# Moving half of the first attention phase of an eight-phase transformer kernel into the chunks of the phase behind it

## What is computed

```python
x = x + tanh(g_xattn[0]) * xattn0(layernorm(x), ctx)      # phase 0
x = x + tanh(g_ffn[0]) * ffn0(layernorm(x), Wr, Wg, Wu, Wd)   # phase 1

def xattn0(Q, K):                 # per block; no softmax
    scores = tril(ones) * (K @ K.T)
    return Q + scores @ Q

def ffn0(x, Wr, Wg, Wu, Wd):      # 8 experts of 256 hidden, top 2
    combine = softmax over the top 2 of x @ Wr, scattered to 8
    return sum over e of (silu(x @ Wg[e]) * (x @ Wu[e]) @ Wd[e]) * combine[e]
```

## Time and profile before

| | |
|---|---|
| median of 3 runs | 873.83 us |
| the runs | 873.89, 866.33, 873.83 us |
| the profiled execution | 869.13 us, of which its span is 867.3 us |
| TensorE busy | 824.7 us, 95% of the span |
| VectorE, ScalarE, GpSimd busy | 515.7, 407.0, 471.2 us |
| mean granted TensorE clock | 0.985 of full speed |

### The profile page before, as it was taken

The page is one execution under the profiler, slowest core; times in us unless marked ns, Lnnn a source line. Parts: engine busy times, 40 slices in busy tenths (PEclk is TensorE's granted clock), DMA queues, the critical chain, the costliest instruction groups (busy, mean ns, idle before and its releaser), DMA issues.

```text
span 867.3 us, 13578 instructions
## 1 busy us (share of the span) xinstructions
PE 824.7 (95%) x4427; PEld 560.2 (65%) x4427; DVE 515.7 (59%) x1444; ACT 407.0 (47%) x730; POOL 471.2 (54%) x449
## 2 busy tenths in 40 slices
PE   5999999998899999999998999999999988999997
PEld 5866676665566666665765666656566665666664
DVE  6866645584865646335555868686755466556431
ACT  2343353634436242325666676756556633424231
POOL 5585757465573747476444343354545248475553
PEclk9999999999999999999999999999999899999999
DMA  8303111214313142441323131322223024424251
GB/s 317 104 15 99 63 36 32 85 43 154 119 44 119 62 129 67 136 124 35 89 83 107 46 89 42 95 50 50 55 49 93 1 67 134 147 66 148 75 154 50
DMA packets 44727, 75.29 MB, mean 87 GB/s; under 512 B 8977, under 2 KB 9361, under 8 KB 44529
## 3 DMA queue, kind: packets, MB, share of 16 engines
q1 hardware_dynamic: 44512, 74.42, 28.4%
q10 hardware_dynamic: 144, 0.01, 0.0%
HBM read 56.11 MB, written 1.51 MB: 66 GB/s over the span
## 4 chain that ended last, share of the span: by engine, by line
PE 56%; DVE 9%; ACT 3%; issue 2%; POOL 0%; ACTq 0%; DVEq 0%; POOLq 0%
PE Y L930 13%; PE B L857 6%; PE B L855 6%; PE B L856 6%; PE B L1498 5%; PE B L1517 3%; PE B L1479 3%; PE B L1485 2%; PE Y L1370 2%; PE B L1478 2%; DVE mxh L1768 1%; PE T L1303 1%; DVE xhat L1752 1%; DVE bcs L1943 1%; ACT shared L1379 1%
## 5 line engine op out<-in xcount | busy, mean ns | idle before, releaser
L1172 POOL TENSOR_TENSOR shared<-shared,bcs 128x512 f32<-128x512 f32 x192 | 247.4, 1293 | 195.8 <-DVE shared L1209 177.0
L1209 DVE TENSOR_TENSOR shared<-shared,B 128x512 f32<-128x512 f32 x204 | 139.5, 686 | 206.4 <-PE B L857 160.4
L1058 ACT ACTIVATE shared<-B 128x512 f32<-128x512 f32 x204 | 121.7, 598 | 280.0 <-PE B L857 279.5
L930 PE MATMUL Y<-shared,down_lo 128*128 128x512 f32 x408 | 209.1, 598 | 0.0
L1712 POOL TENSOR_TENSOR shared_r<-shared_r,const 128x512 fp32r<-128x512 f32 (+1 forms) x128 | 116.4, 940 | 80.3 <-PE B L1479 61.8
L1768 DVE TENSOR_REDUCE mxh<-B 128x4 fp32r<-128x512 f32 (+1 forms) x128 | 78.9, 618 | 82.2 <-PE B L1479 81.5
L1648 ACT COPY shared<-B 128x512 f32<-128x512 f32 (+1 forms) x128 | 64.7, 505 | 61.6 <-PE B L1498 61.5
L1638 ACT ACTIVATE shared<-B 128x512 f32<-128x512 f32 (+1 forms) x128 | 69.6, 544 | 48.9 <-PE B L1485 47.6
L930 PEld LDWEIGHTS Y<-shared,down_lo 128*128 128x128 f32 x408 | 72.5, 190 | 21.1 <-issue 9.5
L855 PE MATMUL B<-shared_r,gate_hi 128*128 128x512 f32 x102 | 80.9, 794 | 0.0
L855 PE MATMUL B<-x_lo_r,gate_hi 128*128 128x512 f32 x102 | 77.6, 761 | 0.4 <-ACT shared L1058 0.4
(11 more groups left out here) (306 smaller groups left out, 1469.8 us busy)
## 6 DMA issues: line engine op xcount, KB each, us to landing
bcs<-wrow SPq DMA_DIRECT2D x96, 256.0 KB, 3.8
shared_r<-shared_r SPq DMA_DIRECT2D x256, 64.0 KB, 2.0
bcs<-wrow SPq DMA_DIRECT2D x128, 128.0 KB, 2.9
gate_lo<-in_moe SPq DMA_DIRECT2D x9, 256.0 KB, 5.3
up_lo<-in_moe SPq DMA_DIRECT2D x9, 256.0 KB, 5.5
down_lo<-in_moe SPq DMA_DIRECT2D x9, 256.0 KB, 4.3
small<-in_small SPq DMA_DIRECT2D x1, 1372.5 KB, 11.7
X<-in_x SPq DMA_DIRECT2D x4, 256.0 KB, 5.2
```

What stands on the lines that cost most here:

```text
L930: nc.tensor.matmul(Y[:], w_raw[2][:, at:at + P], hid[(n0 + c) % HIDDEN], start=(i == 0), stop=(i == m["NC"] - 1))\
L1058: nc.scalar.activation(sg[(n0 + n) % ACTIVE], B[n % GATES][:], ACT.Silu).then_inc(sem("sg_ready"), 1)
L1172: gp.tensor_tensor(hid[(n0 + n) % HIDDEN], hid[(n0 + n) % HIDDEN], bcs[(PLACE.k0[p] + r // m["PER"]) % BROADCAST], ALU.mult)\
L1209: nc.vector.tensor_tensor(hid[(n0 + n) % HIDDEN], sg[(n0 + n) % ACTIVE], up[:], ALU.mult)\
```

## The change

Groups 0 and 1 of phase 0 stay in front of the first chunk; groups 2 and 3 move inside the first seven chunks of phase 1. On PE the scores of group 2 come behind chunk 0 and its result behind chunk 2, the scores of group 3 behind chunk 3 and its result behind chunk 5. Both use bank B5 for the scores and Y for the result. The normalising of groups 1, 2 and 3 goes from DVE to ACT (`p0_apply`: an activation with a scale and a bias for each partition, four for a group), for which DVE also writes the negated mean and POOL multiplies it by the inverse root (`offset0`). The casts of pieces 2 and 3 move behind the first four SiLUs on ACT; the subtractions of pieces 2 and 3 move from DVE to POOL, the last of them behind weighted chunks 1 and 2. POOL's four tiles of group 1 (`apply(run.step(1), ...)`) move from ahead of the chunks to one behind each of weighted chunks 0 to 3. The gate and up weights of each piece are loaded right behind the group's context, and the down weights behind all of them with semaphores of their own.

```diff
-        xhat0, sm = ([area0.tile([P, TG]) for g in range(NG)] for _ in range(2))
+        xhat0, sm = ([area0.at_tile(i + g, [P, TG]) for g in range(NG)] for i in (15, 19))
...
+        neg_mean0 = sb("neg_mean0", [P, NG, GB])
+        offset0 = sb("offset0", [P, NG, GB])
+        SCORE0, OUT0 = (B[0], B[1], B[5], B[5]), (Y, B[4], Y, Y)
+
+        def p0_scores(pe, g):
+            pe.wait_ge(sem(f"ctx_loaded{g}"), 16)
+            if g == 3:
+                pe.wait_ge(sem("p0_masked"), 3)
+            for j in range(GB):
+                kt = context(g, j)
+                ins = nc.tensor.matmul(SCORE0[g][:, j * P:(j + 1) * P], kt, kt, start=True, stop=True)
+            ins.then_inc(sem("p0_scores"), 1)
+
+        def p0_result(pe, g):
+            pe.wait_ge(sem("p0_masked"), g + 1)
+            pe.wait_ge(sem("p0_xhat"), g + 1)
+            if g >= 2:
+                pe.wait_ge(sem("p0_updated"), (1, 3)[g - 2])
+            for j in range(GB):
+                o, q = OUT0[g][:, j * P:(j + 1) * P], xhat0[g][:, j * P:(j + 1) * P]
+                nc.tensor.matmul(o, sm[g][:, j * P:(j + 1) * P], q, start=True, stop=False)
+                ins = nc.tensor.matmul(o, ident, q, start=False, stop=True)
+            ins.then_inc(sem("p0_out"), 1)
...
-            for g in range(NG):
-                scores(g)
-            result(0)
-            result(1)
+            p0_scores(pe, 0)
+            p0_scores(pe, 1)
+            p0_result(pe, 0)
+            p0_result(pe, 1)
             norm_pe(pe, 0, 0)
-            result(2)
             pe.wait_ge(sem("first_loaded"), 16)
             route_pe(pe, 1)
-            result(3)
...
+            if g:
+                v.tensor_scalar(neg_mean0[:, g, :], mv0[:, g, :, 0], -1.0, None, ALU.mult)
+            v.tensor_scalar(var0[:, g, :], mv0[:, g, :, 1], LN_EPS, None, ALU.add).then_inc(sem("p0_var"), 1)
...
-            statistics(0)
-            statistics(1)
-            apply(0)
-            mask(0)
-            apply(1)
-            mask(1)
-            statistics(2)
+            p0_statistics(dve, st, 0)
+            p0_mask(dve, 0)
+            dve.wait_ge(sem("p0_rstd"), 1)
+            for j in range(GB):
+                ins = nc.vector.tensor_scalar(xhat0[0][:, j * P:(j + 1) * P], token_tile(0, j),
+                                              mv0[:, 0, j, 0:1], rstd0[:, 0, j:j + 1], ALU.subtract, ALU.mult)
+            ins.then_inc(sem("p0_xhat"), 1)
+            p0_statistics(dve, st, 1)
+            p0_mask(dve, 1)
             dve.wait_ge(sem("tgate_ready"), 1)
-            update(0)
+            p0_update(dve, 0)
             norm_stats(st, 0)
-            statistics(3)
             norm_apply(dve, 0, 0, 0)
-            apply(2)
-            mask(2)
-            apply(3)
-            mask(3)
+            p0_statistics(dve, st, 2)
             x_low_dve(dve, 1)
-            update(1)
-            update(2)
+            p0_update(dve, 1)
             for _ in route_dve(dve, st, 1):
                 pass
-            update(3)
+
...
+        def p0_apply(act, g):
+            act.wait_ge(sem("p0_offset"), g)
+            if g == 1:
+                act.wait_ge(sem("p0_xhat"), 1)
+            for j in range(GB):
+                ins = nc.scalar.activation(xhat0[g][:, j * P:(j + 1) * P], token_tile(g, j), ACT.Identity,
+                                           bias=offset0[:, g, j:j + 1], scale=rstd0[:, g, j:j + 1])
+            ins.then_inc(sem("p0_xhat"), 1)
 
         def p0_act(act):
-            for q in range(2):
-                for k in range(2):
-                    weights_hi(act, 1, q, k)
+            p0_apply(act, 1)
+            for k in range(2):
+                weights_hi(act, 1, 0, k)
             norm_act(act, 0, 0)
             x_high_act(act, 1)
             for k in range(2):
-                weights_hi(act, 1, 2, k)
+                weights_hi(act, 1, 1, k)
             scores_act(act, 1)
-            for k in range(2):
-                weights_hi(act, 1, 3, k)
...
+                if g:
+                    pool.wait_ge(sem("p0_rstd"), g + 1)
+                    gp.tensor_tensor(offset0[:, g, :], neg_mean0[:, g, :], rstd0[:, g, :], ALU.mult)\
+                        .then_inc(sem("p0_offset"), 1)
 
             power0(0)
             power0(1)
-            power0(2)
+            power(0)
             for k in range(2):
                 weights_lo(pool, gp, 1, 0, k, "w_lo1")
-            power(0)
+            power0(2)
+            for q in (1, 2):
+                for k in range(2):
+                    weights_lo(pool, gp, 1, q, k, "w_lo1")
             power0(3)
-            pool.wait_ge(sem("p0_masked"), NG)
-            for k in range(2):
-                weights_lo(pool, gp, 1, 1, k, "w_lo1")
...
-                    if i == a and p == 1 and q >= 2:
-                        pe.wait_ge(sem("w_lo1_dve"), 2 * (q - 1))
-                    elif i == a:
+                    if i == a:
                         pe.wait_ge(sem(f"w_lo{p}"), 2 * (q + 1))
...
+                    if p == 1 and n in (0, 3):
+                        p0_scores(pe, 2 + n // 3)
                     if (p, n) == (1, 2):
                         turn(1, 0)
+                    if p == 1 and n in (2, 5):
+                        p0_result(pe, 2 + n // 5)
...
-                if (p, n) == (1, 1):
+                if (p, n) == (1, 2):
                     turned_act(act, 1)
...
+                if p == 1 and n in (0, 4):
+                    p0_apply(act, 2 + n // 4)
+                if p == 1 and n < 4:
+                    weights_hi(act, 1, 2 + n // 2, n % 2)
...
-            apply(run.step(1), range(GB))
+            if run is STREAMS[1]:
+                apply(run.step(1), range(GB))
...
+                if p == 1 and n < GB:
+                    apply(run.step(1), (n,))
+                if p == 1 and n in (1, 2):
+                    weights_lo(pool, gp, 1, 3, n - 1, "w_lo1")
...
-                norm_stats(st, 1)
...
-                if p == 1 and n in (1, 2, 3, 4):
-                    weights_lo(dve, nc.vector, 1, 2 + (n - 1) // 2, (n - 1) % 2, "w_lo1_dve")
+                if p == 1 and n in (1, 4):
+                    p0_mask(dve, 2 + n // 4)
+                if p == 1 and n in (3, 6):
+                    p0_update(dve, 2 + n // 6)
+                if (p, n) == (1, 1):
+                    norm_stats(st, 1)
+                if (p, n) == (1, 2):
+                    p0_statistics(dve, st, 3)
...
                 sp.dma_start(CT[:, c], ctx_d[:, c]).then_inc(sem(f"ctx_loaded{g}"), 16)
+                for k in range(2) if g else ():
+                    sp.dma_start(w_raw[k][:, piece(1, g - 1)], moe_d[1][k][:, piece(1, g - 1)])\
+                        .then_inc(sem(f"raw1_{g - 1}"), 16)
+            for k in range(2):
+                sp.dma_start(w_raw[k][:, piece(1, 3)], moe_d[1][k][:, piece(1, 3)]).then_inc(sem("raw1_3"), 16)
             for q in range(NG):
-                for k in range(3):
-                    sp.dma_start(w_raw[k][:, piece(1, q)], moe_d[1][k][:, piece(1, q)]).then_inc(sem(f"raw1_{q}"), 16)
+                sp.dma_start(w_raw[2][:, piece(1, q)], moe_d[1][2][:, piece(1, q)]).then_inc(sem(f"raw_down1_{q}"), 16)
```

78 lines of the change are left out of this document (28 added, 50 removed).

## The result

| | kernel before | kernel changed |
|---|---|---|
| median of 22 runs each, taken in turn | 873.12 us | 877.0 us |
| ratio of the times, 95% interval | | 1.0049, 1.0028 to 1.007 |
| the profiled execution, its span | 869.13, 867.3 us | 876.9, 875.1 us |
| mean granted TensorE clock | 0.985 | 0.983 |
| transposes of group 1 begin | 44.11 us | 48.05 us |

The change costs 4.3 us by the ratio (2.4 to 6.1); the two medians are 3.9 us apart. The forecast was 873 us, level with the kernel before, and it expected the transposes of group 1 at 45.9. They come 3.95 us later than before instead of 1.8.

The account below looks back on a forecast made before the run. TensorE was taken to bound the kernel, with gaps at the start. A 7.6 us lead less 5.4 us of returned work and later waits came to +1.8 us: 870.9 or 875.6, middle 873 us, range 866 to 879.

Parts of the forecast that it names:

- Until chunk 0: Start of the kernel: with group 0 alone first and apply at 1.1 us, chunk 0 at 19.9 us against 27.53.
- T1: Start of the transposes of group 1 in the one profiled execution; forecast at 45.9 us against 44.11.
- 16.8 and 19.9: Start of the kernel: forecast times in us of the transposes of group 0 and of chunk 0's first matmul.
- the tiles' 1.04 us: Price of one GpSimd normalising tile when VectorE works beside it, against 0.81 us alone.
- The routing: VectorE's step behind x_lo and update of group 1: 3.2 us, VectorE free at 23.8, SiLU 0 at 24.0.
- PE's wait for the result of group 2: Behind chunk 2 and the transposes of comb: PE stands 2.0 us until VectorE's mask of group 2 at 28.5.
- GpSimd's tiles last: Ahead of group 1's transposes: tiles ready at 45.9, PE waits 1.9 us, +1.8 us; as a rival, +0.5 to +3.5, chance 0.50.
- The two unmeasured prices: Operations without a trace row: ACT's four 128x128 activations, 1.55 us together, and POOL's 4-column offset, 0.5 us.
- The table load: Between ACT's exponential and SiLU 0: 1.28 us with nothing behind it; by the skill's drain, 1.4 us more.
- rival 3: Clock falls again in waits ahead of group 2's result or for the tiles: +4.0 us, 877 on forecast's scale; chance 0.13.
- The level: Base for the +1.8 us: 870.9 from the profiled execution, 875.6 from the median; the middle, 873 us, was predicted.

Follow-up runs that it names:

- e1_hold: Changed kernel plus one wait: GpSimd's subtractions of weight piece 0 wait for VectorE's normalised x of group 0; 875.9 us, ratio 1.0045 to the kernel before.
- h2_after_ride_held: Changed kernel plus one wait in phase 3: GpSimd waits until VectorE has written the riding attention's four tiles; 868.76 us, ratio 0.9948 to the kernel before.
- f1: Kernel before without GpSimd's wait for the four phase 0 masks ahead of piece 1's subtractions; 877.94 us, ratio 1.0041 to the kernel before.
- g4: Kernel before plus one wait in phase 3: GpSimd waits until VectorE has written the riding attention's four tiles; 866.48 us, ratio 0.9899 to the kernel before.
- k2: The same kernel as g4, run again on another chip; 868.27 us, ratio 0.9931 to the kernel before.
- g1: f3 with GpSimd's subtractions of pieces 0 and 1 back where the changed kernel has them, without waits for VectorE; 872.33 us, ratio 0.9975 to the kernel before.
- f3: Changed kernel with its start reordered on GpSimd, ScalarE, TensorE and VectorE, with subtractions held apart from VectorE's normalising; 867.93 us, ratio 0.9927 to the kernel before.
- f2: e2 with one VectorE setup copy rewritten to read PSUM and the other moved to an earlier step; 872.71 us, ratio 0.9992 to the kernel before.
- e2: Changed kernel with GpSimd's four tiles of group 1 back ahead of the weighted chunks; 881.31 us, ratio 1.0093 to the kernel before.
- e3: Changed kernel plus 19 unread 128x128 matmuls in TensorE's idle time around the transposes of group 0; 878.71 us, ratio 1.0073 to the kernel before.
- e4: Changed kernel with the normalising of groups 2 and 3 back on VectorE, behind products 0 and 4; 881.02 us, ratio 1.0109 to the kernel before.
- h1_probe: Kernel before plus three stretches behind its end of twelve back-to-back GpSimd instructions each, beside VectorE work; ran once, 912.82 us, no ratio.

## Why the prediction was wrong

- **Until chunk 0: the failed step.** "Update, statistics, power and apply then take what they took." The apply was priced at the 1.1 us of the earlier trace rows, which it had beside a mere power (18.35 us, four columns), the subtractions being over by 16.86. The change itself set the subtractions on the same instant, as the order of GpSimd showed, and the walk costed GpSimd's instructions only as time on GpSimd. It took 3.01, 1.9 us more; the forecast missed T1 by 2.15. With the hold (e1_hold) the forecast's 16.8 and 19.9 are met within 0.1, and T1 comes at 46.22 instead of 48.05. The prediction did allow for contention once, in the tiles' 1.04 us "when VectorE works beside it", but not the other way round.
- **The routing.** SiLU 0 was forecast at 24.0 and came at 26.99: 1.9 us from L245, 1.0 from the small copy beside the subtractions of piece 1 (1.17 instead of 0.17). These 2.9 us are more than T1 missed; 0.7 came back on GpSimd, where the offset took 0.20 instead of 0.5 and the chunks and tiles 10.7 instead of 11.1.
- **PE's wait for the result of group 2** was there, ended by the mask as said, 1.51 us instead of 2.0. From that result to T1 TensorE needed 15.8 us without the last wait, forecast 15.4.
- **GpSimd's tiles last: right.** Weighted chunk 0 to the last tile's end took 10.7 us, forecast 11.1, and TensorE waited for it, 0.75 us instead of 1.9, since TensorE too was late. The two unmeasured prices were near: 1.65 us for four activations (1.55), 0.20 and once 0.59 for the offset (0.5).
- **The table load.** 25.70 + 1.28 = 26.98, and SiLU 0 starts at 26.99. The row was right to be taken, not the drain that the Trainium skill gives beside the load (page "ScalarE: Activation LUTs", section "What ACT_TABLE_LOAD costs").
- **The clock (rival 3).** It did not fall in the two waits that the rival named. It fell at 16.1 us, 2.4 us earlier than before, and was at half for 10.2 us instead of 6.8; with 3.4 us of it the same start had the same T1 (h2_after_ride_held, 47.93). That the rival named 877 us is chance.
- **The level: the second failed step.** The sum was +1.8 us. It was put on the kernel's own profiled time (870.9) and on its median (875.6), and the middle was taken, 873, which is no change against the median. A difference belongs on the median: 873.12 + 1.8 = 874.9. With L245's 1.9 it is 876.8, beside the 877.0 measured, but that the two meet proves nothing: e1_hold has L245 at 1.11 and is still 3.5 us over the kernel before. Nor does it speak for the account that 877.0 lies between 866 and 879, since that range was drawn wide enough for the spread of single runs.
- **What stays open.** That keeping the two engines apart saves time is shown by runs that change one wait (f1, g4 and k2 against the kernel before, clear of the noise) and borne out by g1 against f3 and by f2 against e2, which also moves a copy. For the changed kernel itself the undoing of L245 showed in the start and not in the median, so how its 4.3 us divide between L245 and the chain is the account of one profile, not of the times.

## What to carry to other kernels

When a change moves work on GpSimd, lay its timeline beside VectorE's: a two-input GpSimd instruction beside a VectorE instruction that goes from SBUF to SBUF was a wait for VectorE here, until that instruction's end at least (1.3 us for 128x512). A plain wait that holds GpSimd back, or an input read from PSUM, can be worth more than the idle time it costs (g4_before_ride_held, f2_tiles_copies), and a wait that looks needless may be doing just that. Put a predicted difference on the median, and look at more than one profiled execution before believing a difference of 2 us in it.

## What the runs showed of the hardware

VectorE's tiles (four of 128x128, SBUF to SBUF) took 3.01 to 3.06 us beside two subtractions in all eight profiles in which they met (the kernel changed, e2, e3, e4 twice, f1, f2, g1, h2), and 1.10 to 1.12 where they did not meet. Touched too was x_lo, with two SBUF inputs (1.13 instead of 0.69 in e1_hold). Not touched were statistics (bn_stats, 0.86 us for four at 31.37 beside a subtraction in the kernel changed) and the forms with a PSUM input (0.69 us in every stretch of h1_probe). The Trainium skill, page "SBUF — State Buffer", section "Who interferes with whom", says that VectorE and GpSimd share a pair of ports under an exclusive lock, held for a whole instruction, that a copy or tensor_scalar of VectorE may want and that two SBUF inputs want too. The traces agree with who is touched. GpSimd pays as well: the subtraction at 22.61 in the earlier trace rows, beside VectorE's x_lo, took 1.65 us in the kernel before, g4, k2 and h1_probe, where the next one took 1.26 or 1.27.

The same page's "for the whole instruction" would bound a wait by one GpSimd instruction, 1.3 us. The probe agrees (1.08 to 1.33), and the program does not: copies of 6.43 and 6.81 us, each past five boundaries of GpSimd, and a tile of 2.90 past one; the copy of 6.81 took 0.43 in another execution of the same program.

The lock also differs from profile to profile. Without the hold in phase 3 the four tiles there took 4.80 to 4.82 us in ten profiles and 2.15 in two; in h1_probe, which is the kernel before up to its end, they took 3.33 where the kernel before had 4.81. f2_tiles_copies was 3.1 us later in its start, met these places better and ended no later.
